# A fused image embedding, attention and expert layer: router steps and row scatters reordered, the experts' second product from rounded pieces

## The chip, the cores and the metric

One core of a Trainium2 chip runs the whole kernel. The time is the device time of one execution in microseconds (us). TensorE (PE), VectorE (DVE), ScalarE (ACT), GpSimd (POOL) and SyncE (SP) each work through their own list of instructions in order and wait for one another on semaphores.

## The reference, cut to what matters

```python
h = patch_sums(x) @ channel_weights            # 64 images, 196 tokens of 192 values
h = concatenate([h, txt], axis=1)              # + 32 text tokens: T = 228 tokens an image
h = h + attention(layernorm(h))                # 12 heads of 16, rotary, causal, a sink
xf = layernorm(h)                              # 14592 tokens
probs = softmax(xf @ gate_w.T); top_p, top_i = top_k(probs, 2)
pos = running number of the token within its expert; keep = pos < cap      # cap = 4560, 8 experts
buf[expert, pos] = xf[token]
z = 2 * buf * rsqrt(mean((2 * buf)**2) + eps) * norm_w[expert]
g, u = split(z @ w13[expert].T)                # 192 -> 2 x 512
y = buf + (silu(g) * u) @ w2[expert].T         # 512 -> 192
out = h + sum over the 2 choices of weight * y
```

## The kernel before

It has two passes. The first has 64 images and runs 68 steps, a pipeline over images in which each step works on up to five of them at once: `p` (the newest: image folded and pooled), `a` (first layer norm and q, k, v), `m` (scores for the row maxima), `t` (scores again, exponential, product with the values) and `z` (the oldest: output projection, second layer norm, router). `step_tensor`, `step_scalar`, `step_vector` and `pass1_gpsimd` write out by hand the order of the pieces of work of a step on each engine; nothing else orders them. On PE a "ring" of 24 groups (S0 to S8 transposed scores of `t`, C0 to C8 scores of `m`, T0 to T5 transposes of `a`) uses four PSUM banks in turn: a group may start when the engine that reads the group four places earlier has done so (`bank_free`).

The pieces that matter here: on DVE `norm1_stats`, `max_scores` ("maxima", nine of them, each reads one C group), `residual` and `norm2_stats`, `pool_image` (three, each reads what POOL's `fold_image` made), `rotate` (two, each reads what PE's `make_qk` made), `choose` (the two best experts from PE's `gate_logits`), `make_shift` (needs all nine maxima; PE's `turn_shift` waits for it), `assign` (slots of the rows, from PE's `rank`) and `weigh` (weights of the rows). On POOL `inverse_std` (for `a` with norm 1, for `z` with norm 2), `fold_image`, `add_rotation`, `low_parts`, `spread_patches` and `scatter_rows`, four indirect DMAs that write the rows of `z` to their experts' slots in `moe_rows`. On ACT `norm1_apply` normalizes `a` and PE's `turn_xn` transposes it. Before the change `assign` stands after `make_shift`, and `weigh` after `split_shift`.

The second pass takes the slots of each expert in ten tiles of 456 rows, 80 tiles in all, in pairs (`par` 0 and 1 have a buffer each). PE does for each tile four `expert_up(j)` (ten matmuls of 456 columns each, operands in fp32r pieces), `turn_z` of the next tile, then `expert_down`. ACT's `silu` and DVE's `make_hid` make the hidden values between. DVE's `weigh_rows` makes the weighted output rows and POOL's `add_rows` adds them to `out` by four accumulating indirect DMAs. DVE's `take_numbers` copies the next tile's row numbers and weights into the buffer from which those DMAs of two tiles ago took theirs, so it waits for their landing (`added`). Before the change this wait stands ahead of `weigh_rows` of the tile in hand, and `add_rows` waits for the landing of the tile before. Rows that only fill an expert's slots have a number past the tokens and are added to spare rows of `out`.

Of the kernel before, what the change touches and what calls it, by code (L numbers as in the profile page):

```python
# [25 lines left out]
D = 192  # L26
# [6 lines left out]
C = D // 2  # L33
# [91 lines left out]
def build(nc, x, txt, chan_w, norm_scale, norm_bias, w_attn, b_attn, w_proj, b_proj, sinks,  # L125
# [17 lines left out]
    with ctx:  # L143
# [29 lines left out]
        b_row = sb("b_row", [1, 3 * D])  # L173
        b_fold = sb("b_fold", [1, 3 * D])
# [25 lines left out]
        rot_s = sb("rot_s", [TT, 2, 2 * D])  # L200
        qk = sb("qk", [TT, 2, 2 * HEADS, 4, HD], fp32r)
# [67 lines left out]
        nw = sb("nw", [128, 2])  # L269
        w_hi, w_lo = ([pieces[:, 4 * HID * i:4 * HID * (i + 1)].rearrange("p (a n) -> p a n", a=2) for i in pair]  # L270
# [75 lines left out]
        gate_up = [sem(f"gate_up{j}") for j in range(4)]  # L346
        silued = sem("silued")
        hid_made = [sem(f"hid_made{j}") for j in range(4)]
# [7 lines left out]
        def setup_sync(sp):  # L356
            for dst, src in (
# [6 lines left out]
                (b_row[:, :], b_attn.rearrange("(a n) -> a n", a=1)),  # L364
# [32 lines left out]
            sp.dma_start(w_qkv[C:C1, 1, :], b_fold[:, :]).then_inc(bias_placed, 16)  # L397
# [649 lines left out]
        def step_tensor(pe, p, a, m, t, z):  # L1047
# [18 lines left out]
            if t:  # L1066
                attend(pe, t, 0)
# [12 lines left out]
            if z:  # L1080
                rank(pe, z)
            ring("S8 C7 C8")
# [16 lines left out]
        def step_scalar(act, p, a, m, t, z):  # L1099
# [5 lines left out]
            exps("0")  # L1105
            if a:
                norm1_apply(act, a)
            exps("1 2")
            if a:
                copy_xn(act, a)  # L1110
            exps("3")
            if z:
                norm2_apply(act, z)
            exps("4")
            if z:
                copy_xf(act, z)
            if a:
                high_parts(act, a, 0)
            if m:
                keep_h(act, m)  # L1120
            exps("5")
            if z:
                exp_gap(act, z)
            exps("6")
# [18 lines left out]
        def step_vector(dve, p, a, m, t, z):  # L1143
# [16 lines left out]
            maxima("3")  # L1160
            if p:
                pool_image(dve, p, 1)
            if a:
                rotate(dve, a, 1)
            maxima("4 5")
            if z:
                choose(dve, z)
# [6 lines left out]
            if z:  # L1174
                assign(dve, z)
# [4 lines left out]
            if z:  # L1180
                weigh(dve, z)
# [51 lines left out]
        def pass1_gpsimd(pool):  # L1233
            def one(half, par, known=None, fill=None):
# [3 lines left out]
                if p:  # L1238
                    fold_image(pool, p, 0)
                if z:  # L1240
                    inverse_std(pool, z, norm2)
                if p:
                    fold_image(pool, p, 1)
# [58 lines left out]
        WP = 4  # L1302

        def weight_piece(i):

            return i // 2, slice(HID * (i % 2), HID * (i % 2 + 1))

        def round_expert(act, e, par, i):
            if i == 0:
                act.wait_ge(w_loaded, 112 * (e + 1))  # L1310
                wait(act, down, TILES * (e - 1))
                if isinstance(e, int) and e == 0:
                    act.wait_ge(scored_t[8], B)
            c, cols = weight_piece(i)
            nc.scalar.activation(w_hi[par][:, c, cols], w_raw[:, c, cols], ACT.Copy, scale=nw[:, c:c + 1]).then_inc(w_rounded, 1)

        def split_expert(dve, e, par, i):
            dve.wait_ge(w_rounded, WP * e + i + 1)
            c, cols = weight_piece(i)
            nc.vector.scalar_tensor_tensor(out=w_lo[par][:, c, cols], in0=w_raw[:, c, cols], scalar=nw[:, c:c + 1],  # L1320
                                           in1=w_hi[par][:, c, cols].bitcast(fp32), op0=ALU.mult,
                                           op1=ALU.subtract).then_inc(w_split, 1)

        def piece_of(last, par, j):

            return 2 * par + j - 1 if last and 1 <= j <= 2 else None
# [22 lines left out]
        def take_numbers(dve, n, par, pair, e):  # L1349
# [3 lines left out]
            hold(dve, y_weighted, n - 1, held)  # L1353
# [23 lines left out]
        def round_z(act, n):  # L1377
            act.wait_ge(za_turned, n + 1)
            nc.scalar.activation(za_hi[:, :], bank[4][:, 0:ROWS], ACT.Copy).then_inc(za_rounded, 1)
            act.wait_ge(zb_turned, n + 1)  # L1380
            nc.scalar.activation(zb_hi[:, :], bank[5][:, 0:ROWS], ACT.Copy).then_inc(zb_rounded, 1)

        def split_z(dve, n):

            dve.wait_ge(za_rounded, n + 1)
            nc.vector.tensor_tensor(za_lo[:, :], bank[4][:, 0:ROWS], za_hi[:, :].bitcast(fp32), ALU.subtract).then_inc(za_split, 1)
            dve.wait_ge(zb_rounded, n + 1)
# [4 lines left out]
        def expert_up(pe, n, e_par, j):  # L1392
# [4 lines left out]
            if j >= 2:  # L1397
                pe.wait_ge(hid_made[j - 2], n + 1)
            else:
                wait(pe, hid_made[j + 2], n)  # L1400
# [9 lines left out]
            ins.then_inc(gate_up[j], 1)  # L1410

        def silu(act, n, j):
            act.wait_ge(gate_up[j], n + 1)
            if j >= 2:
                act.wait_ge(hid_made[j - 2], n + 1)
            else:
                wait(act, hid_made[j + 2], n)
            nc.scalar.activation(act_g[:, j % 2, :], bank[2 * (j % 2)][:, 0:ROWS], ACT.Silu).then_inc(silued, 1)  # L1418

        def make_hid(dve, n, j):  # L1420
            dve.wait_ge(silued, 4 * n + j + 1)
            if j == 0:
                wait(dve, down, n)
            nc.vector.tensor_tensor(hid[:, j, :], bank[2 * (j % 2) + 1][:, 0:ROWS], act_g[:, j % 2, :], ALU.mult).then_inc(hid_made[j], 1)  # L1424

        def expert_down(pe, n, e_par):
            wait(pe, y_weighted, n)
            for j in range(4):
                pe.wait_ge(hid_made[j], n + 1)
                for s in range(SUB):  # L1430

                    ins = nc.tensor.matmul(bank[6 + s // 2][0:TT, D * (s % 2):D * (s % 2 + 1)], hid[:, j, TT * s:TT * (s + 1)],  # L1432
                                           w_dn[e_par][:, j, :], start=(j == 0 and s % 2 == 0), stop=(j == 3),
                                           skip_group_check=True)
# [16 lines left out]
        def add_rows(pool, n, par, pair):  # L1451
            pool.wait_ge(y_weighted, n + 1)
            pool.wait_ge(numbered, n + 1)

            if par:
                hold(pool, added[0], 16 * SUB * (pair + 1), held)
            else:
                hold(pool, added[1], 16 * SUB * pair, held)
            for s in range(SUB):
                nc.gpsimd.indirect_dma_start(  # L1460
                    out=out[:, :], out_offset=bass.IndirectOffsetOnAxis(ap=who[par][:, s:s + 1], axis=0),
                    in_=ys[par][:, s, :], in_offset=None, bounds_check=TOKENS + ROWS - 1, oob_is_err=True,
# [4 lines left out]
        def over_tiles(eng, tile, between=None):  # L1467


            def expert(e, e_par):  # L1470
                def pair_of(k):
                    pair = e * PT + k
                    last = isinstance(k, int) and k == PT - 1
                    for par in range(2):
                        tile(2 * pair + par, e, e_par, par, pair, last)
# [4 lines left out]
                with eng.Fori(1, PT - 1) as k:  # L1480
                    pair_of(k)
                pair_of(PT - 1)
# [14 lines left out]
        def _(sp):  # L1497
# [11 lines left out]
            def tile(n, e, e_par, par, pair, last):  # L1509
# [13 lines left out]
        def _(pool):  # L1523
# [9 lines left out]
            def tile(n, e, e_par, par, pair, last):  # L1533
                inverse_rms(pool, n + 2)
                add_rows(pool, n, par, pair)
# [6 lines left out]
        def _(dve):  # L1542
# [6 lines left out]
            split_z(dve, 0)  # L1549
# [3 lines left out]
            def tile(n, e, e_par, par, pair, last):  # L1553
                n1, par1, pair1 = ahead(n, par, pair)
                make_hid(dve, n, 0)
                make_z(dve, n1, par1)
                for j in range(1, 4):
                    make_hid(dve, n, j)
                    piece = piece_of(last, par, j)
                    if piece is not None:  # L1560
                        split_expert(dve, e + 1, 1 - e_par, piece)
                split_z(dve, n1)
                take_numbers(dve, n1, par1, pair1, e + 1 if last and par else e)
                mean_square(dve, n + 2)
                weigh_rows(dve, n, par)

# [80 lines left out]
```

## Time and profile before

| | us |
|---|---|
| median of 3 runs (lowest, highest) | 3116.91 (3115.43, 3157.16) |
| the profiled execution | 3111.47 |
| its span, first to last instruction | 3109.3 |
| PE busy | 2852.4 (92%) |
| DVE busy | 1827.3 (59%) |
| ACT busy | 1497.5 (48%) |
| POOL busy | 2019.5 (65%) |

Busy shares are over the whole span and mix both passes. PE's granted clock was 0.978 of full speed in the mean.

### The profile page before, as it was taken

The numbers are of one execution on the slowest core, as the hardware profiler recorded it, in microseconds if no ns is written. First come the engines' busy times: TensorE is split into PE (matmuls) and PEld (weight loads), VectorE is DVE, ScalarE is ACT, GpSimd is POOL, SyncE is SP. The second block draws the span as 40 slices with busy tenths as digits, with TensorE's granted clock in tenths as the row PEclk, the third lists the DMA queues.
The fourth block names the chain that finished last, engine by engine and source line by source line (L and its number), as shares of the span: only waits on it lengthen the run. The fifth ranks groups of instructions, "written<-read, shape, count | busy, mean of one in ns | idle before, by whom it ended". The sixth has DMA issues, their size and how long they took to land.

```text
span 3109.3 us, 62400 instructions
## 1 busy us (share of the span) xinstructions
PE 2852.4 (92%) x20432; PEld 2539.9 (82%) x20432; DVE 1827.3 (59%) x5319; ACT 1497.5 (48%) x3736; POOL 2019.5 (65%) x2070
## 2 busy tenths in 40 slices
PE   1899999999999999999999985999999999999997
PEld 0788888888888888888878875989898989888997
DVE  2466766676676766677766753444444545444544
ACT  0455555555555555555555553444443444344433
POOL 2567877777777777777777742555565555555555
PEclk9899999999999999999999997999999999999999
DMA  6354445433444433444433303343333343433343
GB/s 182 131 165 156 152 162 172 146 101 101 114 115 115 108 95 104 115 115 115 110 96 102 84 23 74 54 68 48 68 54 68 47 68 54 67 49 66 54 67 44
DMA packets 205961, 297.49 MB, mean 96 GB/s; under 512 B 88374, under 2 KB 167675, under 8 KB 205874
## 3 DMA queue, kind: packets, MB, share of 16 engines
q1 hardware_dynamic: 82994, 243.82, 27.4%
q0 software_dynamic: 122880, 52.55, 12.0%
q8 instruction: 50, 0.82, 0.1%
q14 instruction: 37, 0.30, 0.0%
HBM read 201.73 MB, written 93.90 MB: 95 GB/s over the span
## 4 chain that ended last, share of the span: by engine, by line
PE 32%; issue 22%; POOL 19%; DMA 14%; DVE 6%; ACT 4%; POOLq 1%; DVEq 1%; SPq 0%; ACTq 0%
DMA out<-arena,who 13%; POOL out L1460 10%; PE bank L861 6%; POOL moe_rows L1281 5%; PE bank L979 3%; PE bank L927 3%; DVE arena L1442 3%; PE bank L952 2%; PE bank L954 2%; PE bank L905 2%; PE bank L1029 2%; POOL rstd L706 2%; PE bank L963 1%; PE bank L852 1%; PE bank L929 1%
## 5 line engine op out<-in xcount | busy, mean ns | idle before, releaser
L1460 POOL DMA_INDIRECT out<-arena,who x320 | 596.1, 1863 | 187.4 <-issue 183.2
L1281 POOL DMA_INDIRECT moe_rows<-row,slot x256 | 293.2, 1145 | 349.0 <-issue 324.8
L570 DVE TENSOR_REDUCE top<-bank 114x2 f32<-114x456 f32 (+1 forms) x576 | 352.9, 622 | 240.9 <-PE bank L921 153.4
L1418 ACT ACTIVATE arena<-bank 128x456 f32<-128x456 f32 x320 | 174.9, 547 | 602.4 <-PE bank L1409 600.8
L685 POOL TENSOR_TENSOR arena<-arena 112x896 f32<-112x896 f32 x192 | 402.2, 2096 | 44.4 <-DMA arena<-in_x 44.4
L1432 PE MATMUL bank<-prob,arena 128*114 128x192 f32 x2560 | 429.3, 326 | 0.0
L1432 PEld LDWEIGHTS bank<-prob,arena 128*114 128x114 f32 x2560 | 412.2, 178 | 0.0
L1424 DVE TENSOR_TENSOR arena<-bank,arena 128x456 f32<-128x456 f32 x320 | 201.5, 630 | 209.3 <-ACT arena L1418 207.3
L1449 POOL TENSOR_TENSOR rms<-rms,minus_half 114x4 f32<-114x4 f32 x82 | 85.3, 1040 | 345.3 <-DVE rms L1347 345.3
L725 POOL TENSOR_TENSOR qk<-rot_c,qk 114x384 fp32r<-114x384 f32 x256 | 253.7, 1014 | 44.4 <-ACT qk L746 44.4
L547 ACT ACTIVATE pieces<-bank 64x456 fp32r<-64x456 f32 x384 | 209.2, 545 | 149.3 <-PE bank L905 147.1
L1405 PE MATMUL bank<-pieces 128*128 128x456 f32 x640 | 258.7, 404 | 23.9 <-DVE arena L1424 16.7
L804 ACT ACTIVATE prob<-bank 115x456 f32<-115x456 f32 x384 | 207.7, 541 | 151.1 <-PE bank L955 150.4
L1354 DVE COPY w_slot<-arena 114x4 f32 (+1 forms) x81 | 13.8, 170 | 395.2 <-DMA out<-arena,who 395.1
L1409 PE MATMUL bank<-pieces 128*128 128x456 f32 x640 | 237.7, 371 | 0.0
L1407 PE MATMUL bank<-pieces 128*128 128x456 f32 x640 | 237.3, 371 | 0.0
L1408 PE MATMUL bank<-pieces 128*128 128x456 f32 x640 | 237.2, 371 | 0.0
L1406 PE MATMUL bank<-pieces 128*128 128x456 f32 x640 | 236.6, 370 | 0.0
L501 DVE TENSOR_REDUCE pooled<-arena 112x14 f32<-112x896 f32 x192 | 206.5, 1075 | 23.8 <-POOL arena L685 23.8
L905 PE MATMUL bank<-ident_r,qk 114*128 114x114 f32 x1536 | 202.2, 282 | 9.7 <-POOL qk L725 9.7
L905 PEld LDWEIGHTS bank<-ident_r,qk 114*128 114x128 f32 x1536 | 186.5, 196 | 22.1 <-POOL qk L725 19.6
L861 PE MATMUL bank<-w_qkv,xn_t 97*114 97x384 f32 x512 | 200.7, 516 | 2.5 <-DVE rot_s L534 1.8
(167 smaller groups left out, 6971.3 us busy)
## 6 DMA issues: line engine op xcount, KB each, us to landing
arena<-in_x SPq DMA_DIRECT2D x64, 2352.0 KB, 11.6
arena<-moe_rows SPq DMA_DIRECT2D x82, 363.4 KB
moe_rows<-filler SPq DMA_DIRECT2D x20, 1453.5 KB
out<-h SPq DMA_DIRECT2D x64, 171.0 KB
out<-arena,who POOLq DMA_INDIRECT x320, 5.0
arena<-in_w_t SPq DMA_DIRECT2D x9, 512.0 KB, 6.7
arena<-in_w_t SPq DMA_DIRECT2D x18, 256.0 KB, 7.1
moe_rows<-row,slot POOLq DMA_INDIRECT x256, 4.1
```

The source lines that it names most:

```text
L570: nc.vector.tensor_reduce(dst, src, AX.X, ALU.max).then_inc(maxed[k], 1)
L685: nc.gpsimd.tensor_tensor(xin[at.par][:, g, 0:mid], xin[at.par][:, g, 0:mid], xin[at.par][:, g, mid:XF], ALU.add).then_inc(x_folded, 1)
L725: ins = nc.gpsimd.tensor_tensor(lo, of, first.bitcast(fp32), ALU.subtract)
L861: ins = nc.tensor.matmul(bank[6][0:TT, 0:2 * D], xn_t[:, c, TT * t:TT * (t + 1)], w_qkv[:, c, 0:2 * D], start=(c == 0), stop=(c == 1))
L905: ins = nc.tensor.matmul(dst[:, TT * (2 * pair + half):TT * (2 * pair + half + 1)], src, ident_r[0:TT, 0:TT], start=True, stop=True)
L1281: nc.gpsimd.indirect_dma_start(out=moe_rows[0:SLOTS, :], out_offset=bass.IndirectOffsetOnAxis(ap=slot[at.par][:, 2 * t + k:2 * t + k + 1], ...
L1405: nc.tensor.matmul(dst, hi[:, 0, col], za_hi[:, :], start=True, stop=False)
L1407: nc.tensor.matmul(dst, lo[:, 0, col], za_hi[:, :], start=False, stop=False)
L1408: nc.tensor.matmul(dst, hi[:, 1, col], zb[:, :], start=False, stop=False)
L1409: ins = nc.tensor.matmul(dst, lo[:, 1, col], zb[:, :], start=False, stop=True)
L1432: ins = nc.tensor.matmul(bank[6 + s // 2][0:TT, D * (s % 2):D * (s % 2 + 1)], hid[:, j, TT * s:TT * (s + 1)], w_dn[e_par][:, j, :], start= ...
L1460: nc.gpsimd.indirect_dma_start(out=out[:, :], out_offset=bass.IndirectOffsetOnAxis(ap=who[par][:, s:s + 1], axis=0), in_=ys[par][:, s, :], ...
```

## The change

Pass 1. PE: C2 now stands ahead of `turn_xn`; `attend 0` ahead of `make_qk 0`; `turn_xf` ahead of C3 and S4; `gate_logits` right behind `make_qk 1`, ahead of C4 and S5; `rank` ahead of S7 and C6. ACT: exponential 1 ahead of `norm1_apply`; the router's pieces one to three places earlier; `keep_h` later. DVE: `choose` ahead of the second `rotate` and of maxima 4 and 5; that `rotate` ahead of `pool_image` 1; `assign` and `weigh` behind maximum 5, ahead of maxima 6 to 8 and `make_shift`. POOL: `inverse_std` of `z` ahead of the first `fold_image`.

Pass 2. `expert_down` works from pieces: ACT rounds the hidden values to fp32r (`high_hid`), DVE subtracts (`low_hid`), and the second product is high x high + high x low + low x high in fp32r, 48 matmuls in place of 16 in fp32. The second weights are split in the same way (two more pieces an expert; the pieces are spread over the last two pairs of tiles). `take_numbers` stands behind `weigh_rows`; `add_rows` waits for earlier landings only at an expert's first tile; numbers past the tokens are dropped by the DMA. The last two pairs of an expert are written out behind its loop, in place of the last one. Counting semaphores take the place of lists of four.

```diff
@@ step_tensor
-            ring("S1 C1 S2")
+            ring("S1 C1 S2 C2")
             if a: turn_xn(pe, a)
-            ring("C2 S3")
+            ring("S3")
+            if t: attend(pe, t, 0)
             if a: make_qk(pe, a, 0)
-            if t: attend(pe, t, 0)
-            ring("C3 S4")
             if z: turn_xf(pe, z)
+            ring("C3 S4")
             if a: make_qk(pe, a, 1)
-            ring("C4 S5")
             if z: gate_logits(pe, z)
-            ring("C5 S6")
+            ring("C4 S5 C5 S6")
             if t: attend(pe, t, 1)
-            ring("S7 C6")
             if z: rank(pe, z)
-            ring("S8 C7 C8")
+            ring("S7 C6 S8 C7 C8")
@@ step_vector
             if a: rotate(dve, a, 0)
             maxima("3")
+            if z: choose(dve, z)
+            if a: rotate(dve, a, 1)
+            maxima("4")
             if p: pool_image(dve, p, 1)
-            if a: rotate(dve, a, 1)
-            maxima("4 5")
-            if z: choose(dve, z)
+            maxima("5")
+            if z: assign(dve, z); weigh(dve, z)
             maxima("6")
             if p: pool_image(dve, p, 2)
             maxima("7 8")
             if m: make_shift(dve, m)
-            if z: assign(dve, z)
             if a: place_k(dve, a, 1)
             if m: split_shift(dve, m)
-            if z: weigh(dve, z)
@@ pass1_gpsimd
                 if a: inverse_std(pool, a, norm1)
-                if p: fold_image(pool, p, 0)
                 if z: inverse_std(pool, z, norm2)
-                if p: fold_image(pool, p, 1)
+                if p: fold_image(pool, p, 0); fold_image(pool, p, 1)
@@ pass 2
+        def high_hid(act, n, j):
+            act.wait_ge(hid_made, 4 * n + j + 1)
+            nc.scalar.activation(hid2[:, j, 0, :], hid[:, j, :], ACT.Copy).then_inc(hid_high, 1)
+        def low_hid(dve, n, j):
+            dve.wait_ge(hid_high, 4 * n + j + 1)
+            nc.vector.tensor_tensor(hid2[:, j, 1, :], hid[:, j, :], hid2[:, j, 0, :].bitcast(fp32), ALU.subtract)
         def expert_down(pe, n, e_par):
             for j in range(4):
-                pe.wait_ge(hid_made[j], n + 1)
+                pe.wait_ge(hid_low, 4 * n + j + 1)
                 for s in range(SUB):
-                    nc.tensor.matmul(dst, hid[:, j, at], w_dn[e_par][:, j, :])
+                    for part, (h_part, w_part) in enumerate(((0, 0), (0, 1), (1, 0))):
+                        nc.tensor.matmul(dst, hid2[:, j, h_part, at], w_dn2[e_par][:, j, w_part, :])
@@ add_rows
-            if par: hold(pool, added[0], 16 * SUB * (pair + 1), held)
-            else: hold(pool, added[1], 16 * SUB * pair, held)
+            if first:
+                wait(pool, added[0], 16 * SUB * pair); wait(pool, added[1], 16 * SUB * pair)
-            bounds_check=TOKENS + ROWS - 1, oob_is_err=True
+            bounds_check=TOKENS - 1, oob_is_err=False
@@ a tile on DVE
-                make_hid 0; make_z; make_hid 1, 2, 3; split_z; take_numbers; mean_square; weigh_rows
+                make_hid 0; make_z; make_hid 1; low_hid 0, 1; make_hid 2; low_hid 2; make_hid 3
+                split_za; low_hid 3; split_zb; mean_square; weigh_rows; take_numbers
```

## Rows read from the trace of the kernel before

**Rows 1.** Windows: length, busy us of PE, PEld, DVE, ACT, POOL; granted clock, DMA.
```profile
1197.35:1224.62 27.27, 25.04 (x218) 21.92 (x217) 19.39 (x58) 15.08 (x34) 20.71 (x27) 1.00 0.41 109
1904.73:3076.08 1171.35, 1149.34 (x6321) 1057.89 (x6321) 565.86 (x1527) 485.93 (x1455) 663.39 (x391) 0.99 0.37 59
2247.76:2261.97 14.21, 14.21 (x82) 13.45 (x81) 7.15 (x19) 5.83 (x18) 8.47 (x5) 1.00 0.34 52
2601.05:2615.76 14.71, 14.57 (x82) 13.28 (x81) 6.83 (x19) 5.96 (x18) 8.48 (x5) 1.00 0.33 50
```
**Rows 2.** Timeline of PE in pass 1: start us, us, line, x count, [idle before <-releaser].
```profile
1210.73 0.92 PE L1029 MATMUL bank<-gate,xf_t 96*114 96x8 f32 x8
...
1218.84 0.39 PE L938 MATMUL bank<-ident,shift 114*128 114x114 f32 x2 [0.32 <-DVE slot L674]
...
1224.62 0.45 PE L952 MATMUL bank<-pieces 128*115 128x456 f32 x1
...
1230.54 0.63 PE L852 MATMUL bank<-ident,xn 114*97 114x114 f32 x4 [1.34 <-ACT xn L761]
```
**Rows 3.** The chain that ended last, in order of time, pass 1: `make_qk`.
```profile
1208.51 1.29 PE bank L861 x4
```
**Rows 4.** Timeline of POOL in pass 1.
```profile
1204.03 0.20 POOL L704 TENSOR_TENSOR var<-mv,ln_eps 114x2 f32<-114x2 f32 x1
...
1205.51 2.09 POOL L685 TENSOR_TENSOR arena<-arena 112x896 f32<-112x896 f32 x1
...
1222.41 1.20 POOL L1281 DMA_INDIRECT moe_rows<-row,slot  x1 [4.24 <-issue]
```
**Rows 5.** Timeline of DVE in pass 1, the last two rows from its last step.
```profile
1206.38 0.56 DVE L532 TENSOR_TENSOR rot_c<-bank,cos 114x384 f32<-114x384 f32 x1 [0.24 <-PE bank L861]
1206.86 0.55 DVE L534 TENSOR_TENSOR rot_s<-bank,sin 114x384 f32<-114x384 f32 x1
...
1212.66 0.23 DVE L619 MAX8 best<-bank 114x8 f32<-114x8 f32 x2
...
1213.88 0.19 DVE L635 TENSOR_REDUCE counts<-hot 114x16 bf16<-114x32 f32 x1
...
1214.96 1.07 DVE L501 TENSOR_REDUCE pooled<-arena 112x14 f32<-112x896 f32 x1
1215.95 1.16 DVE L570 TENSOR_REDUCE top<-bank 114x2 f32<-114x456 f32 x2
1217.15 0.60 DVE L577 TENSOR_TENSOR shift<-top,sink_tok 114x48 f32<-114x48 f32 x1
...
1228.79 0.25 DVE L518 BATCH_NORM_AGGREGATE mv<-st 114x2 f32<-114x6 f32 x2 [0.16 <-DVE st L514]
...
1880.80 0.17 DVE L663 TENSOR_SCALAR over<-bank 114x16 f32<-114x16 f32 x1 [0.74 <-PE bank L1043]
...
1882.95 0.17 DVE L656 TENSOR_SCALAR token<-token 114x2 f32<-114x2 f32 x1
```
**Rows 6.** Timeline of PE's weight loads: `sel` in pass 1, `expert_down` in pass 2.
```profile
1210.28 0.48 PEld L963 LDWEIGHTS bank<-shift_t,sel 128*114 128x114 f32 x4
...
2610.60 5.15 PEld L1432 LDWEIGHTS bank<-prob,arena 128*114 128x114 f32 x32
```
**Rows 7.** Timeline of POOL and DVE in pass 2.
```profile
2603.62 1.39 DVE L1442 SCALAR_TENSOR_TENSOR arena<-bank,w_slot,arena 114x192 f32<-114x192 f32 x4
...
2606.13 1.91 POOL L1460 DMA_INDIRECT out<-arena,who  x1 [1.42 <-issue]
...
2617.96 0.17 DVE L1354 COPY w_slot<-arena 114x4 f32 x1 [5.15 <-DMA out<-arena,who]
```
**Rows 8.** The same wait in the third tile of an expert.
```profile
2530.22 0.17 DVE L1354 COPY w_slot<-arena 114x4 f32 x1 [6.78 <-DMA out<-arena,who]
```
**Rows 9.** Groups by line, DVE, 2300 to 3000 us: x count, busy us, mean ns, idle before.
```profile
L1386 DVE TENSOR_TENSOR pieces<-bank,pieces 128x456 fp32r<-128x456 f32 x47 | 29.2, 622 | 0.0
L1320 DVE SCALAR_TENSOR_TENSOR pieces<-arena,nw,pieces 128x512 fp32r<-128x512 f32 x20 | 15.0, 751 | 0.0
```

More of the change, by code:

```diff
@@ L1160, in step_vector @@
             maxima("3")
+            if z:
+                choose(dve, z)
+            if a:
+                rotate(dve, a, 1)
+            maxima("4")
             if p:
                 pool_image(dve, p, 1)
-            if a:
-                rotate(dve, a, 1)
-            maxima("4 5")
+            maxima("5")
             if z:
-                choose(dve, z)
+                assign(dve, z)
+                weigh(dve, z)
             maxima("6")
@@ L1173, in step_vector @@
                 make_shift(dve, m)
-            if z:
-                assign(dve, z)
             if a:
@@ L1242, in one @@
                 if p:
+                    fold_image(pool, p, 0)
                     fold_image(pool, p, 1)
@@ L1472, in pair_of @@
                     pair = e * PT + k
-                    last = isinstance(k, int) and k == PT - 1
+                    first, last = (isinstance(k, int) and k == i for i in (0, PT - 1))
+                    late = k - (PT - 2) if isinstance(k, int) and k >= PT - 2 else None
                     for par in range(2):
-                        tile(2 * pair + par, e, e_par, par, pair, last)
+                        tile(2 * pair + par, e, e_par, par, pair, first, last, late)
                 pair_of(0)
@@ L1507, in _, with tile @@
                 load_rows(sp, par, par)
-            def tile(n, e, e_par, par, pair, last):
+            def tile(n, e, e_par, par, pair, first, last, late):
                 sp.wait_ge(z_made, n + 1)
@@ L1531, in _, with tile @@
             inverse_rms(pool, 1)
-            def tile(n, e, e_par, par, pair, last):
+            def tile(n, e, e_par, par, pair, first, last, late):
                 inverse_rms(pool, n + 2)
-                add_rows(pool, n, par, pair)
+                add_rows(pool, n, par, pair, first and not par)
             over_tiles(pool, tile)
@@ L1548, in _, with tile, weights @@
             make_z(dve, 0, 0)
-            split_z(dve, 0)
+            split_za(dve, 0)
+            split_zb(dve, 0)
             take_numbers(dve, 0, 0, 0, 0)
             mean_square(dve, 1)
-            def tile(n, e, e_par, par, pair, last):
+            def tile(n, e, e_par, par, pair, first, last, late):
                 n1, par1, pair1 = ahead(n, par, pair)
+                def weights(j):
+                    for piece in pieces_of(late, par, j):
+                        split_expert(dve, e + 1, 1 - e_par, piece)
                 make_hid(dve, n, 0)
                 make_z(dve, n1, par1)
[L1557 to L1563, printed above, removed]
+                make_hid(dve, n, 1)
+                low_hid(dve, n, 0)
+                low_hid(dve, n, 1)
+                make_hid(dve, n, 2)
+                weights(2)
+                low_hid(dve, n, 2)
+                make_hid(dve, n, 3)
+                split_za(dve, n1)
+                low_hid(dve, n, 3)
+                split_zb(dve, n1)
+                weights(3)
                 mean_square(dve, n + 2)
                 weigh_rows(dve, n, par)
+                take_numbers(dve, n1, par1, pair1, e + 1 if last and par else e)
             over_tiles(dve, tile)
@@ L1598, in _, with tile @@
             turn_z(pe, 0)
-            def tile(n, e, e_par, par, pair, last):
+            def tile(n, e, e_par, par, pair, first, last, late):
                 if par == 0:
```

147 lines of the change are left out of this document (85 added, 62 removed).

## The prediction

> **What bounds the kernel now.** I read the page first: PE is busy for 92% of the span, which suggests that PE's work sets the time, but a busy share says nothing of who ends the waits that are left. So I cut the span in three with the windows: pass 1 to about 1880 us, a change-over, and pass 2 from 1904.73. Then the waits by total and the timeline of one step and of one tile.
>
> Pass 1: a step takes 27.27 us while PE is busy 25.04 [rows 1]. The largest hole in PE is ahead of `turn_xn`, 1.34 us in one step and somewhat more in the one before it [rows 2]. Followed back: it waits for ACT's normalized rows, these for POOL's `inverse_std`, and POOL is late because its four scatters of the step before began only at 1222.41, after 4.24 us idle [rows 4]. What they waited for is `weigh` on DVE. So there is a cycle through `weigh`, the scatters, `inverse_std`, `turn_xn`, the scores and the maxima, back to `weigh`; it, and not PE's work alone, sets the 27.3 us. A second small hole is ahead of `turn_shift`, 0.32 us, ended by `assign` [rows 2].
>
> Pass 2: the 79 tiles from the first start to the last take 1171.35 us, 14.83 each; one without any wait takes 14.21, with PE busy in all of it, a common one 14.71 [rows 1]. So 0.62 us a tile, 49 us in all, is waiting. In the common tile DVE idled 5.15 us for the landing of a scatter, and only then did `weigh_rows` and the hidden values follow; in the third tile of an expert it is 6.78 [rows 7, 8]. From the end of `weigh_rows` (2603.62 + 1.39 = 2605.01) to the copy that the landing releases (2617.96) are 12.95 us, and the next `weigh_rows` comes right after: this loop takes 14.7 us and paces the common tile.
>
> **The change, pass 1.** Let t be the time since S0 of a step begins on PE (1224.62 [rows 2]). What precedes the projection is not changed, so the second norm's statistics end where they do now: 1228.79 + 0.25, t = 4.42 [rows 5]. From here on I follow what waits for what in the new order.
>
> POOL now does `inverse_std` of `z` first and waits for these statistics: 1205.51 - 1204.03 = 1.48 us, so t = 5.96 with 0.06 for the hand-over; then `fold_image` 0, 2.09, t = 8.05 [rows 4]. DVE's first `pool_image` waits for that (0.99, the distance of two starts in rows 5): 9.04. `rotate` 0 stands behind it, 1206.38 to 1206.86 + 0.55, 1.03: t = 10.07 [rows 5]. PE's `make_qk` 1 may not start earlier, since it overwrites what `rotate` 0 reads, and PE reaches it earlier than now, as `attend` 0 no longer lies between: a new hole, about 0.8 us by the same kind of walk along PE. It takes 1.29 [rows 3], the gate's logits 0.92 [rows 2]: t = 12.28.
>
> DVE stands idle for them, because `choose` is next in its list. What is then queued behind that wait on DVE, all of it ahead of `make_shift`: `choose` 1.41 (1212.66 to 1213.88 + 0.19), `rotate` 1.03, maximum 4 0.58 (half of 1.16), `pool_image` 0.99, maximum 5 0.58, `assign` and `weigh` 2.32 (1880.80 to 1882.95 + 0.17), maximum 6 0.58, `pool_image` 0.99, maxima 7 and 8 1.20, the shift 0.60 [rows 5]. That is 10.28: the shift is ready at t = 22.56, and `turn_shift` starts at about 22.6. From there to the next S0 PE has work that the change leaves alone, 1224.62 - 1218.84 = 5.78 [rows 2]. The step is 28.4 us; short overlaps of neighbouring DVE instructions take perhaps 0.1 off, 28.3 to 28.4.
>
> Against 27.3 now this is +1.05 a step. What was gained on the way: the scatters no longer wait (`weigh` ends at 19.2, while POOL with both `low_parts` and `spread_patches` is busy to about 21.5), they end before the next step's first statistics, and the stall ahead of `turn_xn` is gone, with C2 in its place. But 2.32 us of router and one `pool_image` have been put ahead of the shift, and the first fold behind a norm. In the step of now DVE does `assign` behind the shift, `weigh` beside PE's transposes, and the last stretch after the logits holds only a maximum or two, `choose`, one pooling and the shift. Some 60 steps have `z` and all others in them: +63 us. Bounds: PE with no hole at all would give about 25.7 (27.3 less 1.6 of stalls), -96 us; each of the eighteen terms may be 0.02 to 0.05 us off, which makes +35 to +90.
>
> ACT's moves cost nothing: it is busy 15.08 of 27.27 [rows 1], and its rounding of the rotated parts, which T0 needs, is over at t = 17 by the walk, ahead of POOL's second `low_parts` (19.9). T0 can then start at 20.1 and T2 waits for maximum 7 (21.3); both lie ahead of the 22.6 of the shift, so they add nothing.
>
> **The change, pass 2.** `expert_down` now: 32 records in 5.15 us, (5.15 - 0.18)/31 = 0.160 each, 5.13 in all [rows 6]. After: 48 matmuls in fp32r of 192 columns against 114 stationary columns. The trace of before has no such shape. From below: the loads of 114 columns in a row of short fp32r matmuls follow each other in (0.48 - 0.18)/3 = 0.100 us [rows 6]; from above: 0.160, the width 192 in the product of now. I take 0.100: what a tile of 14.21 us leaves beside `expert_down`, 9.08 us, holds the 40 fp32r matmuls of 456 columns and the transposes, so such a matmul takes less than 0.227 and its width scaled to 192 less than 0.096 [rows 1, 6]; the load is then what limits. 48 x 0.100 = 4.80, -0.33 a tile, -26 us in 80 (+205 with 0.160).
>
> Four subtractions on DVE at 0.63 (0.622, one operand from PSUM, [rows 9]) make 2.5 us: 6.83 + 2.5 = 9.4 of 13.9. Four roundings on ACT at about the same make 5.96 + 2.3 = 8.3 [rows 1]. The round trip: the last hidden values are made about 1.3 us after `expert_up` 3, and rounding and subtraction behind `round_za` and `split_za` end some 2.5 us after the start of the transposes; `expert_down` needs that part only 0.8 + 3 x 1.2 = 4.4 us after it. Hidden by PE's own work, with 1.9 us to spare. The weights' two new pieces are one instruction on each engine in each of two tiles.
>
> The scatters: `take_numbers` now stands behind `weigh_rows`, so `weigh_rows` needs no landing. What is queued behind the wait is `make_hid` 0 of the next tile, which can't start for 1.2 us after `weigh_rows` anyhow, and PE asks for it 0.6 later. The loop becomes 12.95 - 1.8 = 11.2 us against a tile of 13.9: covered, also in an expert's third tile, where the landing is 1.6 later. The wait at an expert's first tile falls behind landings 12.95 us after the last start, less than a tile. Dropped rows cost nothing or less. Of the 49 us waited I leave a quarter, 13, as an estimate for waits in which no landing takes part, and count -36 (bounds -20 and -49).
>
> A rule that speaks against it: `low_hid` has both inputs in SBUF while POOL makes descriptors. The trace of before has such an instruction, the splitting of the weights, in tiles in which POOL is at its scatters: 0.751 us in the mean of 20, for 512 columns [rows 9], no more than the size asks. The Trainium skill (SBUF — State Buffer, Who interferes with whom) says that a DVE instruction with two SBUF inputs contends with a GpSimd instruction that reads SBUF, whoever starts first blocking the other. The row shows no blocking.
>
> **Sum.** 3111.47 + 63 - 26 - 36 = 3112. The profiled execution was 5 us below the median shown, so I name 3115. The change-over is left as it is: the two more weight pieces lie in a wait for the rows.
>
> **Rivals.**
> 1. The maxima's queue doesn't hold: pass 1 neither gains nor loses, because one of the waits at the start of my walk (statistics, fold, pooling) is met sooner. Then only pass 2 counts: 3117 - 62 = 3055. For it: the sum of eighteen terms has to be wrong by 1 us. Against: each hand-over is a real dependence. 17%.
> 2. Pass 1 comes down to PE's work: 25.7 a step, 3117 - 96 - 62 = 2959. For it: the largest wait of now is removed. Against: the walk finds a later chain. 12%.
> 3. The other side, slower. The landing paces pass 2 still: `take_numbers` holds `make_hid` of the next tile. It decides if the stretch from `weigh_rows` to the landing grows from 12.95 to over 15.7 us (13.9 + 1.8); at 16.5 the tile is 14.7 as now. Scatters of two tiles that overlap could do that. Then 3117 + 63 = 3180. 12%.
> 4. The narrow fp32r matmuls take 0.160: 7.7 us in place of 5.13, +2.55 a tile, less the waits of 0.6: 3117 + 63 + 155 = 3335. 4%.
> 5. The blocking of the rule above does occur for the four subtractions: each would wait for one indirect instruction of 1.9 us [rows 7], 9.4 + 7.6 = 17.0 us of DVE a tile, +2.2 on 14.8: 3117 + 63 + 176 = 3356. The skill's section named above is what speaks for it, the splitting of the weights against it. 3%.
>
> **How the numbers follow.** The forecast has 52%. The range 3035 to 3185 takes in rivals 1 and 3 and the forecast's own bounds (3075 to 3150) and leaves out rivals 2, 4 and 5 and some tails. A measurement here can tell 2%, 62 us. Faster by more: rival 2, half of 1, a tail of the forecast, 24%. Slower by more: 4, 5, half of 3, a tail, 17%. Within: 59%.
>
> **What would show it.** In the profile after, pass 1 should have steps of 28.3 us, no wait of ACT's normalization for POOL, a DVE wait ahead of MAX8 for the gate's logits of over 1 us, a PE hole ahead of the second `make_qk` and one ahead of `turn_shift` released by the shift. If the steps are shorter than 27, look at when the first `pool_image` starts after S0. In pass 2 the tiles should take 13.9, with loads in `expert_down` 0.100 apart, and the copy of the numbers waiting without PE waiting. The forecast fails if the two halves, +63 and -62, don't cancel; either alone moves it by 2%.

## The result, and the profile after

| | us |
|---|---|
| before, median of 4 runs (lowest, highest) | 3116.68 (3115.43, 3157.16) |
| after, median of 4 runs (lowest, highest) | 3259.08 (3254.09, 3262.89) |
| ratio after / before, 95% interval | 1.0423, 1.0338 to 1.0508 |
| span of the profiled execution, before and after | 3109.3, 3257.8 |
| mean granted clock of PE, before and after | 0.978, 0.942 |

The change costs 4.2%. Where the runs of a kernel below differ by more than 1.5%, they are given one by one, and kernels are compared by those within 1.5% of the fastest. The windows divide the 4.2%. First the 63 steps between the first and the last `turn_xn` before the change; then, of the kernel after, the same 63 steps, the 79 tiles, and two stretches late in one step (columns as in [rows 1]).

```profile
62.61:1807.28 1744.67, 1620.49 (x13515) 1413.30 (x13515) 1192.94 (x3557) 963.01 (x2166) 1298.93 (x1617) 0.98 0.42 121
```
```profile
62.86:2005.06 1942.20, 1756.38 (x13520) 1529.27 (x13520) 1215.43 (x3557) 1001.24 (x2167) 1301.84 (x1616) 0.92 0.37 109
2106.43:3229.49 1123.06, 1103.22 (x7585) 1035.30 (x7585) 791.33 (x1861) 667.50 (x1788) 663.65 (x392) 0.99 0.35 58
1278.75:1283.65 4.90, 4.90 (x28) 4.79 (x27) 1.46 (x4) 2.12 (x6) 3.99 (x4) 0.65 0.95 256
1283.65:1285.97 2.32, 2.32 (x18) 2.26 (x18) 1.52 (x6) 0.97 (x3) 0.04 (x1) 1.00 1.02 308
```

Pass 1 went from 1744.67 to 1942.20, +197.5 us, 3.1 a step; pass 2 from 1171.35 [rows 1] to 1123.06, -48.3. In pass 1 PE does the same number of matmuls, is busy 136 us longer for them, and idle 62 us longer. Most of the 136 is the granted clock, 0.92 in place of 0.98: that is about (0.08 x 1942) - (0.02 x 1745) = 120 us of PE's time.

The timeline of PE in one step after, from the second `make_qk` to the next S0, answers to [rows 2]:

```profile
1265.69 1.52 PE L862 MATMUL bank<-w_qkv,xn_t 97*114 97x384 f32 x4 [0.83 <-DVE rot_s L535]
...
1272.54 0.46 PE L959 MATMUL bank<-mask_k,ident_r 114*114 114x456 f32 x1 [0.42 <-DVE top L571]
...
1276.20 1.07 PE L906 MATMUL bank<-ident_r,qk 114*128 114x114 f32 x8 [1.08 <-DVE top L571]
1277.64 0.65 PE L906 MATMUL bank<-ident_r,qk 114*128 114x114 f32 x4 [0.37 <-DVE top L571]
1278.50 0.41 PE L939 MATMUL bank<-ident,shift 114*128 114x114 f32 x2 [0.20 <-DVE shift L578]
1278.75 2.05 PE L871 MATMUL bank<-w_qkv,xn_t 97*114 97x192 f32 x8
1280.59 1.49 PE L995 MATMUL bank<-ident,y_t 128*114 128x128 f32 x6
1281.73 2.08 PE L906 MATMUL bank<-ident_r,qk 114*128 114x114 f32 x12
1283.65 2.16 PE L844 MATMUL bank<-chan,spread 112*114 112x192 f32 x12
...
1285.97 0.44 PE L953 MATMUL bank<-pieces 128*115 128x456 f32 x1
```

The reader is to see two things. The hole ahead of `turn_xn` is gone, but four others are there, all released by DVE: 0.42, 1.08, 0.37 and 0.20 us within 6 us, and 0.83 before them. And from `turn_shift` (1278.50) to the next S0 (1285.97) are 7.47 us, where [rows 2] had 5.78 for the same work. The twelve transposes of 1281.73, 1.53 us in the kernel before (the row below), take 2.08: in 1278.75 to 1283.65 the granted clock is 0.65 in the mean, which is 3.4 us at the lower of its two levels, 1.2 GHz. Half of that, 1.7 us, is what the tail took longer (7.47 - 5.78 = 1.69). Behind it the clock is at 2.4 GHz again. Below, "the clock falls" means such a stretch at 1.2 GHz; the trace has 60 of them in the 63 steps after and 12 in the 63 steps before. The stretch from `turn_shift` to the next S0 takes 5.8 us in 61 of the 63 steps before; after the change it takes 7.5 in 48 steps, 10.3 to 10.6 in 8 and 5.8 in 5.

```profile
1220.94 1.53 PE L905 MATMUL bank<-ident_r,qk 114*128 114x114 f32 x12
```

DVE and POOL in the same step, the last row from the start of the next:

```profile
1268.06 0.25 DVE L620 MAX8 best<-bank 114x8 f32<-114x8 f32 x2 [1.98 <-PE bank L1030]
...
1271.59 3.90 POOL L726 TENSOR_TENSOR qk<-rot_c,qk 114x384 fp32r<-114x384 f32 x4
...
1274.37 0.20 DVE L654 CAST row<-token 114x2 uint32<-114x2 f32 x1
1274.60 0.92 DVE L657 TENSOR_SCALAR token<-token 114x2 f32<-114x2 f32 x1
...
1276.97 1.16 DVE L571 TENSOR_REDUCE top<-bank 114x2 f32<-114x456 f32 x2
1278.16 0.28 DVE L578 TENSOR_TENSOR shift<-top,sink_tok 114x48 f32<-114x48 f32 x1
1278.20 1.20 POOL L1278 DMA_INDIRECT moe_rows<-row,slot  x1 [0.56 <-issue]
...
1294.06 1.09 DVE L502 TENSOR_REDUCE pooled<-arena 112x14 f32<-112x896 f32 x1 [2.23 <-POOL arena L686]
```

`choose` waits 1.98 us for the logits, the first pooling 2.23 us for the late fold, and the scatters begin without the 4.24 us of [rows 4]. One line is odd: L657, the last instruction of `weigh`, two numbers a partition, takes 0.92 us here and 0.17 in [rows 5]. It ends at 1275.52; POOL's `low_parts` end at 1271.59 + 3.90 = 1275.49. In 58 of the 64 steps it ends 0.02 to 0.03 us behind `low_parts`.

Pass 2 after, beside [rows 6] and [rows 7], and the wait in an expert's third tile, which answers to [rows 8]:

```profile
2602.51 1.39 DVE L1470 SCALAR_TENSOR_TENSOR arena<-bank,w_slot,arena 114x192 f32<-114x192 f32 x4 [1.71 <-PE bank L1460]
2604.03 0.17 DVE L1365 COPY w_slot<-arena 114x4 f32 x1
...
2611.24 4.88 PEld L1460 LDWEIGHTS bank<-w_dn,hid 128*114 128x114 f32 x48
...
2282.45 0.17 DVE L1365 COPY w_slot<-arena 114x4 f32<-114x4 f32 x1 [3.08 <-DMA out<-arena,who]
```

`weigh_rows` now waits for PE's product and the copy of the numbers for nothing; the loads are (4.88 - 0.18)/47 = 0.100 us apart.

### The profile page after: what moved, and what is told of

Read it like the earlier page. It is cut to its first block and busy times, and to the rows that moved or that the text cites. A ratio compares the mean times of both kernels' runs of the same rounds, so it can differ in the third digit from the quotient of the medians.

```text
span 3257.8 us, 65973 instructions
## 1 busy us (share of the span) xinstructions
PE 2943.5 (90%) x21712; PEld 2633.6 (81%) x21712; DVE 2078.5 (64%) x5657; ACT 1719.6 (53%) x4074; POOL 2022.8 (62%) x2070
## 3 DMA queue, kind: packets, MB, share of 16 engines
q0 software_dynamic: 122880, 47.00, 10.3%
## 5 line engine op out<-in xcount | busy, mean ns | idle before, releaser
L1460 PE MATMUL bank<-w_dn,hid 128*114 128x192 f32 x3840 | 401.9, 264 | 0.0
L1460 PEld LDWEIGHTS bank<-w_dn,hid 128*114 128x114 f32 x3840 | 390.3, 180 | 0.0
L571 DVE TENSOR_REDUCE top<-bank 114x2 f32<-114x456 f32 (+1 forms) x576 | 351.2, 619 | 20.0 <-PE bank L922 13.9
L906 PE MATMUL bank<-ident_r,qk 114*128 114x114 f32 x1536 | 231.8, 299 | 98.5 <-DVE top L571 86.7
L906 PEld LDWEIGHTS bank<-ident_r,qk 114*128 114x128 f32 x1536 | 211.0, 213 | 121.3 <-POOL qk L726 89.1
L705 POOL TENSOR_TENSOR var<-mv,ln_eps 114x2 f32<-114x2 f32 x128 | 25.1, 196 | 388.8 <-DVE mv L519 388.8
L1420 PE MATMUL bank<-pieces 128*128 128x456 f32 x640 | 240.5, 376 | 21.3 <-DVE arena L1437 11.6
L559 DVE CAST pieces<-bank 128x456 fp32r<-128x456 f32 x192 | 120.2, 626 | 201.6 <-PE bank L906 197.8
L1424 PE MATMUL bank<-pieces 128*128 128x456 f32 x640 | 237.8, 372 | 0.0
L1423 PE MATMUL bank<-pieces 128*128 128x456 f32 x640 | 237.4, 371 | 0.0
L1422 PE MATMUL bank<-pieces 128*128 128x456 f32 x640 | 236.6, 370 | 0.0
L1421 PE MATMUL bank<-pieces 128*128 128x456 f32 x640 | 236.3, 369 | 0.3 <-issue 0.2
```

What stands on the lines that cost most here:

```text
L571: nc.vector.tensor_reduce(dst, src, AX.X, ALU.max).then_inc(maxed[k], 1)
L906: ins = nc.tensor.matmul(dst[:, TT * (2 * pair + half):TT * (2 * pair + half + 1)], src, ident_r[0:TT, 0:TT], start=True, stop=True)
L1420: nc.tensor.matmul(dst, hi[:, 0, col], za_hi[:, :], start=True, stop=False)
L1421: nc.tensor.matmul(dst, hi[:, 0, col], za_lo[:, :], start=False, stop=False)
L1422: nc.tensor.matmul(dst, lo[:, 0, col], za_hi[:, :], start=False, stop=False)
L1423: nc.tensor.matmul(dst, hi[:, 1, col], zb[:, :], start=False, stop=False)
```

## Experiments

**The two halves apart.** Each pass of the change was put alone into the kernel before: in the first kernel `step_tensor`, `step_scalar`, `step_vector` and `pass1_gpsimd` are those of the change, in the second everything else is.

> The kernel before with the change of pass 1 alone (order of the pieces on PE, ACT, DVE and POOL). Theory: all of the loss is in pass 1, whose steps go from 27.3 to 30.6 us as in the changed kernel; pass 2 keeps its 14.83 us a tile: 3117 + 200 = about 3310. Rival (the loss comes from pass 2's code or from what it leaves behind, such as memory or code loading): under 3200.

> The kernel before with the change of pass 2 alone. Theory: tiles of 13.82 us without waits and 14.2 in the mean, pass 1 as before with steps of 27.3 us: 3117 - 48 = about 3068. Rival (the faster tiles are a matter of the state in which pass 1 leaves the core): tiles as before, 3117.

Measured: 3313.83 (ratio 1.0657, 1.0613 to 1.0701) and 3049.94 (0.9791, 0.9751 to 0.9831). Windows of the 63 steps and the 79 tiles, of the first kernel and then of the second:

```profile
62.90:2001.64 1938.74, 1753.90 (x13520) 1526.87 (x13520) 1214.04 (x3557) 999.43 (x2167) 1301.69 (x1616) 0.93 0.37 109
2106.37:3277.50 1171.13, 1149.32 (x6320) 1059.31 (x6321) 566.98 (x1527) 486.37 (x1455) 663.56 (x391) 0.99 0.37 59
```
```profile
62.17:1805.42 1743.25, 1620.13 (x13514) 1414.01 (x13514) 1195.08 (x3557) 963.91 (x2166) 1299.64 (x1617) 0.97 0.42 121
1903.44:3021.88 1118.44, 1099.24 (x7584) 1033.19 (x7585) 790.36 (x1861) 665.20 (x1788) 663.41 (x392) 1.00 0.35 58
```

The halves don't touch each other: pass 1 of the change loses its 194 us with the old pass 2, and the new pass 2 gains its 53 us with the old pass 1.

**Filling one hole.** A hole can be filled with matmuls whose result is written again unchanged.

```diff
-            for a in range(4):
+            for a in (0, 1, 2, 3) * (2 if g == 2 else 1):   # attend
```

> The changed kernel with the 16 matmuls of attend 2 done twice (the same result written twice), 0.74 us more work for PE in each step, in the place where PE stands idle for 1.08 us ahead of T0. Theory: the granted clock falls to its lower level for 3.4 us in nearly every step because PE has these holes; with them filled it stays up, the step loses 1.7 us in spite of the work added, to about 28.9, and the run about 100 us, to 3160. Rival 1 (the clock has nothing to do with it; PE's tail is slow for the scatters' DMA traffic or another reason): step of 30.6 as before or 0 to 0.7 more, 3259 to 3300. Rival 2 (the clock falls for the load of PE, not for its holes): more half-speed time, over 3259.

Measured: 3162.93, 3202.01, 3220.55 and 3226.90, against 3254.09 to 3262.89 without the added work. In the profiled run (3202.01) steps of 28.8 to 29.1 us, with a 29.5 now and then, have others of 30.5 to 33.8 between; the granted clock is 0.956. The clock falls 30 times in the 63 steps, where it fell 60 times. More work for PE made the kernel faster in every run, by 52 us at least in the first two, and the clock fell half as often. The theory holds as to its sign; the gain is less than the 100 us forecast.

**The router back behind the shift.**

```diff
             maxima("5")
-            if z: assign(dve, z); weigh(dve, z)
...
             if m: make_shift(dve, m)
+            if z: assign(dve, z)
             if a: place_k(dve, a, 1)
             if m: split_shift(dve, m)
+            if z: weigh(dve, z)
```

> The changed kernel with assign and weigh on DVE back behind make_shift and split_shift. Theory: 2.3 us of router and the 0.75 us for which its last instruction stood still leave the queue ahead of the shift; the shift comes at t = 20.0 instead of 23.0, T0 then waits for POOL's low_parts (about 20), holes shrink, the clock stays up: steps of about 27.3, 3259 - 3.3 x 60 = about 3065. Rival (the first fold behind the second norm is what costs; the router's place doesn't matter): steps of 29 or more, over 3160.

Measured: 3106.56, ratio to before 0.9995 (0.9971 to 1.0020). With pass 2's gain in it, pass 1 still loses some 50 us; steps are 28.0 and 28.2 us in turn, with a 29.5 now and then. My 27.3 was too low, the rival's 29 too high. The queue ahead of the shift was most of the loss. What is left shows in PE's waits of 20 steps, and in T0 of one step:

```profile
PE bank L853 <- ACT xn L762: 24.8, 20, 1.3
PE bank L906 <- POOL qk L726: 8.8, 20, 0.5
PE bank L959 <- DVE top L571: 8.5, 20, 0.4
```
```profile
1215.40 1.55 PE L906 MATMUL bank<-ident_r,qk 114*128 114x114 f32 x12 [0.45 <-POOL qk L726]
```

(The numbers are us in total, times, and the longest.) The largest wait is the old one, ahead of `turn_xn`, 1.24 us a step: with `weigh` behind the shift again the scatters start late again, and the cycle through them is back. T0 waits 0.44 for `low_parts`; the late fold alone isn't behind that, for the second kernel of the last test below, with the fold first, has the same wait.

**The fold first.** In `pass1_gpsimd` of the changed kernel, `fold_image` 0 ahead of `inverse_std` of `z`.

> The changed kernel with POOL's first fold_image back ahead of inverse_std of z. Theory (the walk): fold, first pooling and first rotate come about 1.2 us sooner after S0, PE's second make_qk no longer waits, choose starts at t = 11.5 in place of 12.6, and a step without a fall of the clock takes 27.8 in place of 28.9: with the clock as in the changed kernel 3190, with fewer falls down to 3120. Rival (only the stretch from choose to the shift counts, and choose is held by the logits anyhow): choose at 12.6 and 3259.

Measured: 3216.87, 3329.07, 3395.86 and 3450.91; their clocks are 0.944, 0.905, 0.884 and 0.862, the longer the lower. Only the first can be compared, and one run is too few for a verdict on the fold's place: it is 1% below the changed kernel and above the forecast's 3190. The profile is of the run of 3329.07, so it is read for its steps alone. Windows of an early and a later stretch:

```profile
240.00:560.00 320.00, 297.07 (x2422) 258.33 (x2421) 216.08 (x640) 179.55 (x389) 231.84 (x287) 0.97 0.47 154
1000.00:1600.00 600.00, 567.45 (x3838) 500.81 (x3837) 343.58 (x1010) 285.65 (x613) 366.36 (x455) 0.80 0.32 89
```

In the early stretch steps of 28.2 and 29.8 us alternate, near the 27.8 of the walk. From about 880 us on every step takes 34.13 us at a mean clock of 0.80. What the fold's place is worth is read from the last of the fill experiments, in which the clock stays up.

**One instruction moved.** The increment of the token numbers (L657) behind `make_shift`.

> The changed kernel with one instruction moved: the increment of the token numbers on DVE, 0.17 us alone, stands behind make_shift instead of at the end of weigh. Theory: at its old place it takes 0.92 us because it waits for POOL's low_parts to end, and all maxima behind it wait too; behind the shift it takes 0.17. Then the shift comes 0.75 us sooner: steps of 28.1 where the clock stays up, and 3259 - 45 = 3214 if the clock falls as often, down to 3110 if it no longer does. Rival (the DVE instruction is long for a reason of its own, such as its wait): 0.92 at the new place as well, and 3259.

Measured: 3165.63, 3183.82, 3214.45 and 3216.82, against 3259.08. At its new place it takes 0.47 us in the median: less than 0.92, more than 0.17. POOL is then in the first of its scatters:

```profile
1020.25 0.47 DVE L659 TENSOR_SCALAR token<-token 114x2 f32<-114x2 f32 x1
...
1019.54 1.20 POOL L1282 DMA_INDIRECT moe_rows<-row,slot  x1 [0.31 <-issue]
```

It ends at 1020.72, 0.02 us ahead of the scatter's issue. Where it starts 0.53 to 0.62 us into that issue, as in 12 steps, it takes 0.16; where it starts 0.70 us into it or later, as in 49, it takes until the issue ends. Steps with the clock up are 27.9 to 28.1, against 28.9, but about one in four is 32.9 to 34.0. The direction was right: the queue ahead of the shift is shorter by the whole instruction, wherever it then stands.

**Both holes filled, then the same with the instruction at the end of DVE's step.**

```diff
-            for c in range(2):                              # turn_xf
+            for c in (0, 1) * 3:
-            for a in range(4):                              # attend
+            for a in (0, 1, 2, 3) * (3 if g == 2 else 1):   # 2 in the second kernel
```
and in the second kernel the increment stands behind `place_k(dve, a, 5)`, the end of DVE's step.

> The changed kernel with PE given idempotent work in both places where it has holes: the transposes of turn_xf three times (0.8 us, ahead of the second make_qk) and the matmuls of attend 2 three times (1.5 us, ahead of T0). Theory: half the clock falls went with one hole half filled; with all of it filled the clock stays up, steps take 28.9 us throughout, half-speed time comes down from 380 to under 160 us, and the run takes about 3145. Rival (the falls have another cause, such as the amount of PE's work): as many falls as in the changed kernel or more, and 3259 or over.

> As the run before it, with attend 2 only twice, and the increment of the token numbers moved to the end of DVE's step, where POOL does nothing but its scatters. Theory: the increment takes 0.17 us there, the 0.75 us that it waited for POOL's low_parts leave the queue ahead of the shift, and steps take 28.1 with the clock up: 28.9 - 0.75, 45 us less than the run before. Rival (the low_parts or another wait hold T0 by then, so that the queue isn't what ends last): steps of 28.6 or more.

Measured: 3144.12 (ratio to before 1.0142, 1.0093 to 1.0191) and 3083.22 (0.9931, 0.9899 to 0.9962). The first kernel's windows over most of its pass 1, and late transposes of one step:

```profile
150.00:1900.00 1750.00, 1691.24 (x15607) 1487.25 (x15607) 1178.47 (x3488) 971.90 (x2111) 1258.52 (x1565) 1.00 0.39 114
```
```profile
1270.14 1.53 PE L906 MATMUL bank<-ident_r,qk 114*128 114x114 f32 x12
1271.50 2.16 PE L844 MATMUL bank<-chan,spread 112*114 112x192 f32 x12
```

Granted clock 1.00, the transposes back to 1.53 us, all steps but one between 28.8 and 29.1: 115 us gone by adding some 2.3 us of PE work to every step. In the 63 steps the clock falls 3 times. The rival, that the clock falls for PE's load, is ruled out: the load rose. In the second kernel the increment takes

```profile
L659 DVE TENSOR_SCALAR token<-token x64: 156/158/479, 171.4 to 1907.9; 114x2 f32<-114x2 f32 x64
```

(lowest, median and highest ns), where the changed kernel has 170/925/933, and steps are 27.9 and 28.1 in turn: another 0.95 us a step. It has one repetition of `attend` 2 less than the first; that is not what made it shorter, for the steps at 2.4 GHz are 28.8 to 29.1 with two (the first fill) as with three. At the end of DVE's step, too, POOL is at a scatter's issue: most of the 0.16 us are from starts in its last 0.13 us, and in 14 steps with starts 0.64 to 0.91 us into it the instruction lasts to its end, 0.21 to 0.48.

**The fold first, clock held up.** The last kernel with `fold_image` 0 ahead of `inverse_std` of `z`, and `turn_xf` once.

> As the run before it (attend 2 twice, the token increment at the end of DVE's step), but with POOL's first fold_image ahead of inverse_std of z and turn_xf once, as there is no hole to fill there then. It repeats the test of the fold's place where the clock can't blur it. Theory: choose starts about 0.8 us sooner after S0 and everything behind it too: steps of 27.2 in place of 28.0, clock up, about 3035. Rival (the clock falls anyway, for this order has some other trait that lets it fall): steps of 27.2 mixed with 29 to 34, over 3083.

Measured: 3036.42 (ratio 0.9773, 0.9724 to 0.9822), steps of 27.2, as forecast. The late fold cost 0.8 us a step. The two repetitions of `turn_xf` that went at the same time had cost nothing: steps at 2.4 GHz are the same without them (first fill) and with them (both holes filled). That the order itself makes the clock fall is not so.

**A better version.** If the cycle through `weigh` and the scatters was the bound before, `weigh` need only come a little sooner, not ahead of the shift. Pass 2 of the change, pass 1 of before, and:

```diff
             if m: make_shift(dve, m)
             if z: assign(dve, z)
+            if z: weigh(dve, z)
             if a: place_k(dve, a, 1)
             if m: split_shift(dve, m)
-            if z: weigh(dve, z)
-        gw = bank[7][0:TT, 36:40]
+        gw = sb("gw", [TT, 4])[:, :]
```

> The kernel before with the change of pass 2, and of pass 1 only this: weigh on DVE stands right behind assign, both behind make_shift (its four weights lie in SBUF instead of the PSUM bank that PE writes next). Theory: the scatters start about 1.6 us sooner, so inverse_std and turn_xn do, and the hole of 1.3 to 1.9 us ahead of turn_xn is gone: steps of about 25.9, 3050 - 85 = 2965. Rival (a later chain of about the same length takes its place): steps over 26.8, over 3020.

> The changed kernel with the first fold_image ahead of inverse_std of z, and assign and weigh together right behind make_shift. Theory: neither the queue ahead of the shift nor the late fold is left, and the scatters start early: no hole ahead of turn_xn, steps of about 26, 2970. Rival (the order of the rest of the change still costs something): steps of 27 or more, over 3030.

The second kernel is the whole change with the fold first and this placing of the router. Measured: 2936.30 (ratio to before 0.9447, 0.9391 to 0.9503) and 3000.83 (0.9644, 0.9587 to 0.9701). Steps are 25.4 and 26.6 us; the forecasts, 25.9 and about 26, were too high and too low. The first kernel beats both the kernel before and the changed one; 114 us of it are pass 1's (3049.94 with pass 2 alone). Its windows over pass 1, and its scatter, whose wait is 2.23 us in place of the 4.24 of [rows 4]:

```profile
150.00:1650.00 1500.00, 1491.30 (x12878) 1313.60 (x12876) 1118.81 (x3411) 914.03 (x2057) 1230.23 (x1527) 1.00 0.46 132
```
```profile
1008.74 1.20 POOL L1281 DMA_INDIRECT moe_rows<-row,slot  x1 [2.23 <-issue]
```

PE is busy 1491.30 of 1500 us: only its own work is left. The scatters begin 21.7 us after S0 in the median, where they began at 25.0: 3.3 us sooner, not the 1.6 that I expected. 25.4 is also below the 25.7 that I took for a step without holes. The second kernel has 1.2 us more a step. Its PE waits, in 22 steps, show 0.8 of that:

```profile
PE bank L959 <- DVE top L571: 9.8, 23, 0.4
PE bank L906 <- POOL qk L726: 9.7, 22, 0.5
```

They are two of the waits of the router's test. The first kernel has neither; which of the change's orders makes them was not tried.

## Why the prediction was wrong

I forecast 3115 from +63 and -62 and a range up to 3185; it was 3259.

**What bounds the kernel before: right.** The cycle through `weigh`, the scatters and `turn_xn` set the 27.3 us. Moving `weigh` alone brought 25.4. The forecast's +63 rested on the right new chain as well: in the trace after `choose` starts 12.6 us after S0 in the median (forecast 12.28), released by the logits; PE has its hole ahead of the second `make_qk`, 0.83 (0.8); `turn_shift` is released by the shift, 23.1 us after S0 in the median (22.6).

**What failed: "From there to the next S0 PE has work that the change leaves alone, 5.78".** The work is the same, its duration isn't: 7.47 us in the step shown, 7.5 in 48 of 63 steps and over 10 in 8. I took PE's durations as fixed while moving its holes. The sum foresaw a hole of 0.8 us and put others behind `attend` 2 (T0 at 20.1, the shift at 22.6), and never asked what PE's clock would do. The fill experiments show it: with both holes filled by useless work the clock stays at 2.4 GHz and the mean step falls from 30.83 to 29.04. The clock falls in the kernel before too, at 0.98 in the mean of these steps; the 63 steps after have a clock of 0.92.

**The term "`assign` and `weigh` 2.32": mis-sized.** It came from the last step of pass 1, in which POOL stands idle. At their new place POOL is at `low_parts`, and the last instruction takes 0.92 in place of 0.17. With that instruction out of the queue the step is 0.95 shorter, 0.17 of it its own time. The section behind rival 5 was the one that mattered, and I tried it on the wrong instruction: I asked if the new subtractions of pass 2 are blocked, and let one row of another kind of instruction settle it. For them the answer was right: they take 0.63 in the mean, 0.65 at most. The Trainium skill (SBUF — State Buffer, Who interferes with whom) lists `tensor_scalar` and `copy` among those that can take the port pair shared with GpSimd for a whole instruction, the later one waiting to the end of the earlier. This trace agrees as to `low_parts`: L657 ends 0.03 us after them. It does not as to the scatters: beside an issue of 1.20 us the same instruction took 0.16 us where it started up to 0.62 us into it, and lasted to the issue's end only where it started later.

**The rest of the sum of eighteen terms: about right.** The step with the clock up and the instruction out of the queue is 28.0, with its own 0.17 put back 28.2 (forecast 28.3 to 28.4); the median step before is 27.36.

Taken together, as an estimate from these steps, the 3.1 us that a step takes longer in the mean (27.69 to 30.83) are 0.8 for the queue and the late fold, 0.8 for the blocked instruction, and 1.5 for more falls of the clock. The forecast had only the first, at 1.05. It also left out that rival: all of mine that end slower lay in pass 2.

**Pass 2: right in kind, smaller.** -48 in place of -62. A tile without waits takes 13.82 (forecast 13.9): -0.39 in place of -0.33, 31 us. The waits were mis-sized: 1123.06/79 - 13.82 = 0.40 a tile is left of 0.62, so 17 us were won, not 36. The common tile lost its wait, as forecast. The step that failed is "covered, also in an expert's third tile": the landing there is later than I allowed. The copy waits 3.08 us behind `weigh_rows`, PE 1.3, and the eight third tiles take 15.6 to 18.2 us, 22 us in all above 13.82, about as much as their 23 above 14.21 before. Rival 3's mechanism, the landing that paces the tile, is met there and nowhere else. That the transfer of the next expert's weights delays it was not tried.

**Rivals.** 1 and 2 (pass 1 not slower) fell: the walk's chain was there. 4 fell: 0.100 us a matmul. 5 fell in pass 2; a blocked DVE instruction was found in pass 1, where I had not looked.

## What to carry to other kernels

Moving small dependent instructions ahead of a large engine's gate can cost more than their time: sum what is queued behind them up to the next thing that PE waits for, and shift the late producer by just enough. Here `weigh` right behind the shift was worth 114 us, and 5.5% with pass 2's change; the full move, ahead of the shift, was a loss. Take a duration from a stretch in which the other engines do what they'll do at the new place. And holes in PE can have a second price when the granted clock falls behind them: read the clock's column for the stretch, and fill a hole with repeated matmuls to find out what the clock alone costs.

## What the runs showed of the hardware

A fall of the granted clock in the step shown lasts 3.4 us, at half speed. With holes of 2.9 us in a step of 30.6 there were 60 falls in 63 steps; with both places filled, 3. In one profiled run, of 3329.07 us, the falls became a steady state: with the fold first, steps of 28.2 and 29.8 went over to 34.13 us each at a mean clock of 0.80, and stayed there to the end of the pass. The time of that kernel scatters by 7% from run to run (3216.87 to 3450.91), that of the kernel with one hole filled and of the one with the late increment by 2.0 and 1.6%, that of the kernel before by 1.3%, that of all other variants by less than 1%.

What decides which holes let the clock fall is open. Their sum does not: over the same 63 steps the kernel with the router behind the shift (first row) has PE idle for 147 us and a clock of 0.98, the one with the late increment (second row) has it idle for 126 us and 0.93.

```profile
62.74:1853.02 1790.28, 1642.86 (x13520) 1423.74 (x13520) 1178.11 (x3558) 989.55 (x2167) 1297.81 (x1617) 0.98 0.41 118
```
```profile
62.89:1934.83 1871.94, 1745.98 (x13519) 1518.25 (x13520) 1188.49 (x3557) 992.79 (x2167) 1299.94 (x1616) 0.93 0.38 113
```

One `tensor_scalar` of two numbers a partition took 0.17 us while POOL stood idle, 0.16 where it started up to 0.62 us into a scatter's issue of 1.20, 0.47 where it started 0.70 us into one, and 0.92 beside `low_parts`.
